# Cross-attention and expert FFN on one core: keys and values from high and low parts of ctx

## The reference

```python
xn = layernorm(x)
kp, vp = ctx @ Wk.T + bk, ctx @ Wv.T + bv          # keys, values
x = x + softmax((xn @ Wq.T + bq) @ kp.T / sqrt(128)) @ vp
h = layernorm(x)
probs = softmax(h @ router_w.T)                     # 8 experts
k = argmax(clip(gelu(h @ a1.T + b1) @ a2.T + b2, -30, 30)) + 1
scores = where(rank(probs) < k, probs, 0)
x = x + sum_e scores[e] * (silu(h @ gate_w[e].T) * (h @ up_w[e].T)) @ down_w[e].T
```

## Time and profile before

| | us |
|---|---|
| median of 3 runs | 751.24 |
| lowest, highest run | 751.12, 753.06 |
| span of the profiled execution | 749.5 |
| busy: TensorE, VectorE | 740.2 (99%), 628.6 (84%) |
| busy: GpSimd, ScalarE | 578.4 (77%), 552.9 (74%) |

### The profile page before, as it was taken

One profiled execution on the slowest core, in us unless ns is written; L12 is line 12 of the kernel. 1 busy time (PEld: TensorE's weight loads), 2 busy tenths in 40 slices (PEclk: granted clock), 3 DMA queues, 4 the chain that ended last, 5 costly groups with the idle time before them and its releaser, 6 DMA issues.

```text
span 749.5 us, 13834 instructions
## 1 busy us (share of the span) xinstructions
PE 740.2 (99%) x3721; PEld 366.3 (49%) x3721; DVE 628.6 (84%) x1395; ACT 552.9 (74%) x978; POOL 578.4 (77%) x620
## 2 busy tenths in 40 slices
PE   8999999999999999999999999999999999999998
PEld 5544454544445445454544545445454544544445
DVE  7899888898888888788888888888888887978777
ACT  5998787776877776777776777776777767777664
POOL 2686979789796877969689696886968688687764
PEclk9999999999999999999999999999999999999999
DMA  9200412204032132312224132132313212120110
GB/s 349 66 24 1 84 30 57 58 14 97 25 78 56 49 79 55 84 41 69 70 40 95 40 81 62 42 83 54 82 43 69 72 28 56 32 58 11 28 30 29
DMA packets 107271, 45.40 MB, mean 61 GB/s; under 512 B 86872, under 2 KB 97112, under 8 KB 107224
## 3 DMA queue, kind: packets, MB, share of 16 engines
q1 hardware_dynamic: 106792, 44.39, 24.4%
q10 hardware_dynamic: 432, 0.48, 0.2%
HBM read 26.46 MB, written 10.78 MB: 50 GB/s over the span
## 4 chain that ended last, share of the span: by engine, by line
PE 94%; ACT 3%; DVE 2%; issue 1%; POOL 0%; DVEq 0%; ACTq 0%; POOLq 0%
PE bank L634 28%; PE bank L635 28%; PE bank L636 28%; PE bank L544 2%; PE bank L517 2%; PE bank L630 1%; PE bank L528 1%; PE bank L593 1%; PE bank L612 1%; PE bank L771 1%; DVE bank L1562 0%; ACT up_hi L829 0%; DVE hid_lo L1568 0%; ACT down_hi L829 0%; ACT k_early L890 0%
## 5 line engine op out<-in xcount | busy, mean ns | idle before, releaser
L1207 POOL TENSOR_TENSOR weighted<-silu,score_bc 128x512 f32<-128x512 f32 x336 | 430.9, 1298 | 89.0 <-ACT silu L972 86.2
L1562 DVE SCALAR_TENSOR_TENSOR bank<-bank,h_scale,weighted 128x512 f32<-128x512 f32 x336 | 253.5, 754 | 94.6 <-PE bank L636 76.2
L966 ACT ACTIVATE hid_hi<-bank 128x512 f16<-128x512 f32 x336 | 200.9, 598 | 155.4 <-DVE bank L1562 154.6
L972 ACT ACTIVATE silu<-bank,silu_scale 128x512 f32<-128x512 f32 x336 | 230.7, 687 | 24.3 <-PE bank L636 24.1
L1568 DVE TENSOR_TENSOR hid_lo<-bank,hid_hi 128x512 f16<-128x512 f32 x336 | 227.5, 677 | 0.0
L634 PE MATMUL bank<-xn_lo,gate_hi 128*128 128x512 f16 x336 | 127.5, 379 | 1.1 <-ACT silu L972 1.1
L634 PE MATMUL bank<-xn_lo,up_hi 128*128 128x512 f16 x336 | 127.4, 379 | 1.2 <-DVE hid_lo L1568 0.9
L635 PE MATMUL bank<-xn_hi,up_lo 128*128 128x512 f16 x336 | 127.3, 379 | 0.0
L636 PE MATMUL bank<-xn_hi,up_hi 128*128 128x512 f16 x336 | 127.3, 379 | 0.0
L636 PE MATMUL bank<-xn_hi,gate_hi 128*128 128x512 f16 x336 | 127.3, 379 | 0.0
L635 PE MATMUL bank<-xn_hi,gate_lo 128*128 128x512 f16 x336 | 127.3, 379 | 0.0
(11 more groups left out here) (200 smaller groups left out, 780.3 us busy)
## 6 DMA issues: line engine op xcount, KB each, us to landing
x_in<-in_x SPq DMA_DIRECT2D x16, 256.0 KB, 2.8
y_kept<-y_sb SPq DMA_DIRECT2D x60, 64.0 KB, 2.6
y_tok<-y_kept SPq DMA_DIRECT2D x15, 256.0 KB, 2.8
out<-out_sb SPq DMA_DIRECT2D x15, 256.0 KB, 2.2
xt_in<-in_x_t SPq DMA_DIRECT2D x14, 256.0 KB, 2.8
row_bc<-row_kept SPq DMA_DIRECT2D x14, 256.0 KB, 3.7
ctx_in<-in_ctx_t SPq DMA_DIRECT2D x14, 240.0 KB, 2.7
p_kept<-y_sb SPq DMA_DIRECT2D x10, 256.0 KB, 2.0
```

What stands on the lines that cost most here:

```text
L966: af(hid_hi[j % HRING][:], up_bank[j % U_BANKS][:], ACT.Copy).then_inc(hid_hi_ready, 1)
L972: af(silu[j % RING][:], gate_bank[(par + j) % G_BANKS][:], ACT.Silu, scale=silu_scale[:])\
L1207: g.tensor_tensor(weighted[j % RING][:], silu[j % RING][:], score_bc[par][:], ALU.mult)\
L1562: v.scalar_tensor_tensor(up_bank[j % U_BANKS][:], up_bank[j % U_BANKS][:], h_scale[:], weighted[j % RING][:], ALU.mult, ALU.mult).then_inc ...
```

## The change

From block 6 on (FIRST_SPLIT) keys and values are made from a high and a low part of ctx. ScalarE copies ctx into ctx_hi of the type float32r at tile 3 of turn t for block t + 3, GpSimd subtracts it from ctx into ctx_lo at tile 11, and TensorE makes three float32r products of 480 columns each for the keys at tile 14 and three for the values at tile 17. The two weight matrices are split once, in turn 1. ScalarE's key copy comes at tile 16 instead of 19. The values now come with their channels on the partitions: ScalarE adds the bias while copying them out of bank 6 (tile 18) into v_turn, a piece of the buffer raw[0] that is free by then, VectorE transposes its 32 x 32 squares (tile 19) and SyncE moves them through DRAM into v_sb as `move_probs` does, at the end of its turn. The values are therefore made a turn earlier than before, in turn t for block t + 3. VectorE's bias addition at tile 12 goes. Blocks 6 to 15 have values of the new kind (ten blocks), blocks 7 to 15 keys (nine).

```diff
+FIRST_SPLIT = 6
@@ SyncE
+            def move_values(n):
+                sp.wait_ge(vsq_ready, n - FIRST_SPLIT + 1)
+                sp.dma_start(v_kept, v_sq).then_inc(v_moved, 16)
+                sp.wait_ge(v_moved, 16 * (n - FIRST_SPLIT + 1))
+                for q in range(4):
...
+                    sp.dma_start(v_sb[lo:hi, :].rearrange("r (b i c) -> r b i c", b=BB, i=4),
...
+                        .then_inc(v_in, 16)
@@ SyncE, turn, last
+                if is_split(t + 3):
+                    move_values(t + 3)
@@ TensorE
             def energies(n, dst=x0):
-                wait(pe, x2_ready, n)
+                if is_split(n):
+                    pe.wait_ge(vt_ready, n - FIRST_SPLIT + 1)
+                else:
+                    wait(pe, x2_ready, n)
...
+            def three_products(dst, hi, lo):
+                mm(dst, hi[:], ctx_lo[:], start=True, stop=False)
+                mm(dst, lo[:], ctx_hi[:], start=False, stop=False)
+                return mm(dst, hi[:], ctx_hi[:], start=False, stop=True)
+
+            def split_keys(n):
+                pe.wait_ge(ctx_lo_ready, n - FIRST_SPLIT + 1)
+                pe.wait_ge(kmin_ready, n - 1)
+                three_products(x1[:, 0:NC], key_hi, key_lo).then_inc(kp_done, 1)
+
+            def split_values(n):
...
+                pe.wait_ge(ctx_lo_ready, n - FIRST_SPLIT + 1)
+                pe.wait_ge(x2_ready, n)
+                three_products(x0[:, 0:NC], wv_hi, wv_lo).then_inc(vp_done, 1)
@@ TensorE, turn
-                    if j == 12 and is_block(t + 2) and not is_early(t + 2):
-                        values(t + 2, par)
-                    if j == 12 and is_block(t + 3) and not is_early(t + 3) and not is_ahead(t + 3):
-                        keys(t + 3, nxt)
+                    if j == 14 and is_split(t + 3) and not is_ahead(t + 3):
+                        split_keys(t + 3)
+                    if j == 17 and is_split(t + 3):
+                        split_values(t + 3)
@@ ScalarE
+            def ctx_high(n, par):
+                wait_ctx(act, n, par)
+                act.wait_ge(vp_done, n)
+                af(ctx_hi[:], ctx_in[par][:], ACT.Copy).then_inc(ctx_hi_ready, 1)
+
+            def turned_values(n):
+                act.wait_ge(vp_done, n + 1)
...
+                   x0[:, 0:NC].rearrange("p (b n) -> p b n", b=BB), ACT.Identity, bias=bv_col).then_inc(vt_ready, 1)
@@ ScalarE, turn
-                    if j == 19 and is_block(t + 3) and not is_early(t + 3) and not is_ahead(t + 3):
+                    if j == 3 and is_split(t + 3):
+                        ctx_high(t + 3, nxt)
+                    if j == 16 and is_split(t + 3) and not is_ahead(t + 3):
                         keys(t + 3)
+                    if j == 18 and is_split(t + 3):
+                        turned_values(t + 3)
@@ GpSimd, turn, ahead of route_probs
+                    if j == 11 and is_split(t + 3):
+                        ctx_low(t + 3, nxt)
@@ VectorE
+            def value_squares(n):
+                dve.wait_ge(vt_ready, n - FIRST_SPLIT + 1)
+                wait(dve, v_moved, 16 * (n - FIRST_SPLIT))
+                v.transpose(v_sq, v_turn).then_inc(vsq_ready, 1)
@@ VectorE, turn
-                    if j == 12 and is_block(t + 2) and not is_early(t + 2):
-                        values(t + 2)
+                    if j == 19 and is_split(t + 3):
+                        value_squares(t + 3)
```

More of the change, by code:

```diff
@@ L9 @@
 F16 = mybir.dt.float16
+F32R = mybir.dt.float32r
 U32 = mybir.dt.uint32
@@ L130, in program @@
         key_t, key_col = sb("key_t", [P, P]), sb("key_col", [P, 1])
+        key_hi, key_lo = sb("key_hi", [P, P], F32R), sb("key_lo", [P, P], F32R)
+        wv_hi, wv_lo = sb("wv_hi", [P, P], F32R), sb("wv_lo", [P, P], F32R)
         ones_col = sb("ones_col", [P, 1])
@@ L332, in wait_ctx, with is_split @@
                 eng.wait_ge(ctx_loaded[par], 8 * (n - par) + (16 if isinstance(n, int) and n < 2 else 0))
-        def values_made(n):
-            return n + 1 if isinstance(n, int) and n == 0 else n - 4
+        def is_split(n):
+            return is_block(n) and (not isinstance(n, int) or n >= FIRST_SPLIT)
         def by_tensor(n):
@@ L522, in values @@
                 wait_ctx(pe, n, par)
-                if dst is x0 and is_early(n):
+                if dst is x0:
                     pe.wait_ge(bc_ready, 1)
-                elif dst is x0:
-                    pe.wait_ge(exp_done, n + 1)
                 for b in range(BB):
@@ L536, in attend @@
                     pe.wait_ge(ptt_ready, n + 1)
-                if isinstance(n, int) and n in v_early:
+                if is_split(n):
+                    pe.wait_ge(v_in, 64 * (n - FIRST_SPLIT + 1))
+                elif n in v_early:
                     pe.wait_ge(v_early_ready, n)
                 else:
-                    pe.wait_ge(v_ready, values_made(n))
+                    pe.wait_ge(v_ready, 1)
                 by_half = isinstance(n, int) and n == 0
@@ L625, in keys @@
                     pe.wait_ge(v_raw_ready, 4)
-                elif dst is x1 and not is_early(n):
-                    wait(pe, kmin_ready, n - 1)
                 if isinstance(n, int) and n == 0:
@@ L894, in values, with split_high @@
                 af(v_early[n][:], src[0:CTX, :], ACT.Copy).then_inc(v_raw_ready, 1)
+            def split_high(dst, src):
+                af(dst[:], src, ACT.Copy).then_inc(split_hi_ready, 1)
+            def ctx_high(n, par):
[4 more added lines that the diff above has]
+                act.wait_ge(vp_done, n + 1)
+                wait(act, vsq_ready, n - FIRST_SPLIT)
+                af(v_turn.rearrange("p (b n) -> p b n", b=BB)[:, :, 0:CTX],
+                   x0[:, 0:NC].rearrange("p (b n) -> p b n", b=BB), ACT.Identity, bias=bv_col).then_inc(vt_ready, 1)
             def actor(n):
@@ L1167, in token_low, with ctx_low @@
                     .then_inc(lo_ready, 1)
+            def ctx_low(n, par):
+                pool.wait_ge(ctx_hi_ready, n - FIRST_SPLIT + 1)
+                pool.wait_ge(vp_done, n)
+                g.tensor_tensor(ctx_lo[:], ctx_in[par][:], ctx_hi[:].bitcast(F32), ALU.subtract)\
+                    .then_inc(ctx_lo_ready, 1)
             def route_probs(n):
@@ L1636, in turn @@
                         route_rank(t + 1)
+                    if isinstance(t, int) and t == 1 and j == 14:
+                        split_low(key_lo, key_t[:], key_hi, 1)
+                        split_low(wv_lo, wv_t, wv_hi, 2)
+                    if j == 19 and is_split(t + 3):
+                        value_squares(t + 3)
                     if isinstance(t, int) and t == 0 and j == 0:
@@ L1754 @@
     consts += [rows(L0_xattn_bv), rows(np.arange(KMAX, dtype=np.float32))]
-    consts += [rows(np.tri(EXPERTS, k=-1, dtype=np.float32).reshape(-1))]
+    consts += [rows(np.tri(EXPERTS, k=-1, dtype=np.float32).reshape(-1)), np.asarray(L0_xattn_bv).reshape(P, 1)]
     consts16 = [np.eye(P, dtype=np.float16),
```

17 lines of the change are left out of this document (added).

## The result

| kernel | median us | runs | range | profiled execution | its span |
|---|---|---|---|---|---|
| before | 751.60 | 4 | 751.12 to 753.06 | 751.24 | 749.5 |
| after | 765.38 | 4 | 764.75 to 765.50 | 764.75 | 763.0 |

The ratio of after to before is 1.0184, with a 95% interval of 1.0172 to 1.0196: slower by 13.8 us. The forecast had the sign and the mechanism right and the time inside its range, near its upper end: it expected 8.4 us on the span, and the span grew by 13.5 us. 5.1 us of the cost were not seen. By the prediction's own list the time lies in the bin of a rival, the late transposes (764 to 768 us, given 0.12), and not in the forecast's own 757 to 763 us (0.66).

The account below looks back on a forecast made before the run. TensorE, busy 740.2 of 749.5 us, was taken as the bound. New products 11.5 less 4.1 gained at tile 12, plus 1.0 for SyncE's queue, gave 8.4 us more: 759.6 us, range 755.5 to 766.

Parts of the forecast that it names:

- the late transposes: Rival: transposes land after 3.6 to 4.0 us, TensorE waits 0.5 to 0.9 us before each turn's router product; chance 0.12.
- Point 1: TensorE at tile 12: of 1.68 us removed, 1.22 become waiting for silu; 0.46 gained in nine turns, 4.1 us.
- Point 2: TensorE at tiles 14 and 17: 19 groups of three one-pass products, 0.605 us each, add 11.5 us.
- the 10.4 us: Extra cost on TensorE if three exposed weight loads of 183 ns made a new group 1.15 us instead of 0.60.
- Points 4, 5 and 6: Added or moved copies on ScalarE, subtraction on GpSimd, bias addition swapped for a transpose on VectorE: each cost nothing.
- Point 7: Values' products at tile 17 wait for VectorE's residual of the block before: 0.45 us of slack, cost nothing.
- Point 8: Values' store and loads delay xn_lo's transpose on SyncE; slack falls from 1.07 to 0.2 us; 0.1 us a turn, 1.0 us.
- The bound of 2.0 us a turn: Upper bound of the SyncE queue cost if each transpose landed as late as the longest, 5.1 us; 20 us in all.
- The clock: Rival: TensorE's clock falls in the new waits, costing at most some us; chance under 2%.

Follow-up runs that it names:

- e4: Kernel before with only its two f32 records of keys moved from tile 12 to tile 14; 754.32 us, ratio 1.0041.
- e2: Kernel after with the keys' three products back at tile 12, values staying at tile 17; 759.38 us, ratio 1.0105.
- e7: Kernel after with values and keys both back at tile 12 and the values' DMAs behind those of the probabilities; 748.98 us, ratio 0.9973.
- e1: Kernel after with the gate product of tile 14 put behind up and down at tile 12 in turns 4 to 13 too; 757.44 us, ratio 1.0082.
- e6: Kernel after with the values' three products over 240 columns instead of 480, half of the values left out; 762.04 us, ratio 1.0146.
- e9: Kernel before with only the keys of blocks 7 to 15 as three new-type products at tile 12, values unchanged, no DMAs added; 750.64 us, ratio 0.9993.
- e8: e7 with, in turn 13 alone, the gate product of tile 14 behind up and down of tile 12; 748.08 us, ratio 0.9962.

## Why the prediction was right, and where it was too small

*Point 1, tile 12*: right to the hundredth. The gap forecast from turn 13 of before (silu's start plus 0.74 us, against TensorE's arrival) was 1.22 us, and ten gaps of 1.22 to 1.23 us came. e4 shows the mechanism with no new product, e2 and e7 by filling the gap again. The switch for gate, which the prediction noted as not extended, is worth 7.9 us (e1) of the 12.2; the prediction did not say how much, and the full 12.2 of e1's expectation was too much.

*Point 2, the new products*: one pass was right, the size was 8% too small, 0.655 us a group for 0.605, 0.95 us in all. The step that was off was to take the pace of an f32 record (0.40 us for two passes) for that of the new type. On the weight loads the prediction weighed a rule: the Trainium skill, "TensorE: Matmul & The Clock Gate", section "Weight-path perf modes", leaves FP32 weights without the fast weight load. The loads are indeed long here, 0.19 us against 0.10 for f16, but e6 shows them hidden even behind products of 0.11 us, so nothing of the 10.4 us is paid.

*Points 4, 5 and 6*, ScalarE, GpSimd and VectorE at nothing: the ten gaps did not grow by any copy, and no product waits for what GpSimd or VectorE gained. e1 shows how little was left: with the large gap gone, up of tile 12 waits 0.15 us for VectorE's low half. Its slack in the kernel after was the time for which TensorE stood still and then did the gate product.

*Point 7, the wait at tile 17*: held. Turn 8, VectorE's last residual half and the first product that waits for it, to be set beside the earlier trace rows:

```profile
435.89 0.60 DVE L1515 SCALAR_TENSOR_TENSOR x_all<-bank,inv_sum,x_in 128x128 f32 x2
...
436.76 0.57 PE L582 MATMUL bank<-ctx_lo,wv_hi 128*128 128x480 f32 x1
```

The residual ends at 436.49, 0.27 us before the record starts. As at tile 14, the product streams only when the one ahead of it has, here at 436.95, and read so the slack is 0.46 us, for 0.45 forecast.

*Point 8, SyncE's queue*: the mechanism and the place were right, the term was mis-sized, 1.0 us for 4.4. It put 7.7 us between the start of VectorE's turn of the values and the issue of xn_lo, and left 0.2 us of slack. In turn 8 it was 8.54 us, from 397.49 to 406.03. The chain of waits there (start us, us, what; "SPq L365" is the loop's branch on SyncE):

```profile
397.57 0.63 DVE raw_gate L1509
...
398.21 1.98 DMA v_kept<-raw_gate
...
403.11 0.04 SPq L365
...
403.66 0.37 SPq L466
...
406.03 2.89 DMA xn_lo<-xn_lo
408.92 0.22 issue
```

The store (1.98), the loads (2.85) and the landing (2.89, forecast 2.9) were right. What was set at nothing lies between them: 0.60 us from the last load to the result's store where the loop goes back (turns 6, 8 and 10), 0.39 us in turn 4, 0.21 us in the other turns (449.90 to 450.11 in turn 9), and about 0.2 us more of waits and issues of a few hundredths each up to xn_lo. One more term stood at nothing: the prediction set the landing, 446.9, against the weight load's start, 447.12, as if the product could start on the landing; it starts 0.22 us behind it (408.92 to 409.14), which by itself uses up the 0.2 us of slack in every turn. Each tenth beyond the slack is lost in nine turns. The bound of 2.0 us a turn (landings of 5.1 us) was not touched. Of the rivals, "the transposes come late" is thus the one that came true alongside the forecast, by late issues and not by late landings. That the time also falls into its 764 to 768 us is in part luck: the waits came to 4.4 us where it had 5 to 9, and the products and the rest added 1.75 us that it did not have.

*The clock* did not fall. The window of turn 8 over the wait for silu (the number behind the fifth engine is the granted clock):

```profile
424.30:425.80 1.50, 0.45 (x3) 0.11 (x2) 1.47 (x4) 1.49 (x3) 0.12 (x1) 1.00 0.47 175
```

It stays at 1.00, the 2.4 GHz level, as the earlier trace rows had it.

Open: what causes the small gaps in turn 3, which also stand in e9, and the one in turn 13; and why a gate product behind a new group or a wait for silu holds TensorE 0.009 us longer.

## To carry to other kernels

Before work is taken away from the bounding engine, find the next wait behind that place and the time at which it would end without the work; in a turn that lacks the work already, the trace shows that time exactly. Work moved out of such a place is paid twice, once as idle time where it was and once where it goes, and three passes that fit into the idle time are better left there (e7, e8) than moved to make room. A slack of two tenths that is worked out from a sum over a queue's instructions is no slack: count the queue's waits, branches and issue steps too, and price a shortfall in every turn of the loop.

## What the chip showed that was not expected

- A product whose operands are read in one pass at four bytes takes 0.218 us for 480 columns and 0.11 us for 240 (e6), against 0.216 us for 512 columns of f16: at 480 columns about 0.015 us above the pace of f16.
- SyncE's return through its loop costs about 0.4 us beyond the 0.21 us of a turn without it (0.60 us in turns 6, 8 and 10). While its queue had slack, no product waited for that.
- Giving back 1.2 us a turn at one place (e1) raised three waits of 0.1 to 0.2 us elsewhere, the first of them the same stretch of ScalarE, passed on by VectorE: three engines stand within 0.2 us of each other.
